# Expert routing shared out between GpSimd and VectorE, and weight pieces in other slots, in a two-layer transformer block

## What is computed

```python
x = x + linear_attention(layernorm(x))   # 16 heads of 8, causal
x = x + experts(layernorm(x))
x = x + softmax_attention(layernorm(x))  # 16 heads of 8
x = x + experts(layernorm(x))            # same weights as the first
```

```python
scores = sigmoid(x @ router_w.T)             # 16 per token
s = scores + bias
group_score = top_k(s.reshape(-1, 4, 4), 2).sum(-1)   # 4 groups of 4
gmask = the 2 groups with the highest group_score
idx = top_k(where(gmask, s, -1), 4)
w = scores[idx] / (sum(scores[idx]) + 1e-20) * 2.5
out = sum_e w_e * down_e(silu(x @ gate_e) * (x @ up_e)) + shared
```

## Time and profile before

| | us |
|---|---|
| median of 3 runs | 585.02 |
| lowest and highest | 580.65, 589.15 |
| the profiled execution | 585.89 |
| its span, first to last instruction | 584.2 |
| mean granted clock of TensorE (1 is 2.4 GHz) | 0.955 |
| busy in the span: TensorE, VectorE, ScalarE, GpSimd | 527.8, 439.5, 338.2, 313.0 |

### The profile page before, as it was taken

The page is one execution under the profiler, slowest core; times in us unless marked ns, Lnnn a source line. Parts: engine busy times, 40 slices in busy tenths (PEclk is TensorE's granted clock), DMA queues, the critical chain, the costliest instruction groups (busy, mean ns, idle before and its releaser), DMA issues. The chain is left out here.

```text
span 584.2 us, 11501 instructions
## 1 busy us (share of the span) xinstructions
PE 527.8 (90%) x3757; PEld 395.6 (68%) x3757; DVE 439.5 (75%) x1073; ACT 338.2 (58%) x575; POOL 313.0 (54%) x309
## 2 busy tenths in 40 slices
PE   4888677979999999999888898998999999999996
PEld 3655454667888888888555554655578888888884
DVE  3678679838889798667676787788578797886563
ACT  2566554456555655655455768576855655555553
POOL 4797784436665766677520303111165666656664
PEclk9999995989999999999867999989999999999999
DMA  6359761043353434335632432420153544355350
GB/s 176 100 164 279 226 212 43 4 92 97 102 112 125 128 89 125 90 114 174 205 108 73 138 117 91 127 74 2 39 109 88 121 127 122 101 143 128 91 147 24
DMA packets 48548, 67.59 MB, mean 116 GB/s; under 512 B 6625, under 2 KB 18930, under 8 KB 48498
## 3 DMA queue, kind: packets, MB, share of 16 engines
q1 hardware_dynamic: 45392, 66.47, 39.7%
q10 hardware_dynamic: 3106, 0.48, 0.5%
HBM read 53.56 MB, written 13.37 MB: 115 GB/s over the span
## 5 line engine op out<-in xcount | busy, mean ns | idle before, releaser
L649 POOL TENSOR_TENSOR KS<-PT,QS 128x512 fp32r<-128x512 f32 x144 | 186.0, 1292 | 118.5 <-ACT QS L841 106.5
L836 ACT ACTIVATE bank<-bank 128x512 f32<-128x512 f32 x128 | 74.5, 582 | 99.0 <-PE bank L861 98.5
L1562 DVE TENSOR_TENSOR PT<-CS,bank 128x512 f32<-128x512 f32 x128 | 87.4, 683 | 45.1 <-PE bank L861 44.6
L859 PE MATMUL bank<-XH,WH 128*128 128x512 f32 (+1 forms) x288 | 115.4, 401 | 1.9 <-DVE PT L1434 1.7
L861 PE MATMUL bank<-XH,WL 128*128 128x512 f32 (+1 forms) x288 | 112.8, 392 | 0.0
L860 PE MATMUL bank<-XL,WH 128*128 128x512 f32 (+1 forms) x288 | 112.7, 391 | 0.0
L1459 DVE TENSOR_REDUCE MEXP<-bank 128x4 f32<-128x1024 f32 x64 | 78.2, 1222 | 25.9 <-PE bank L971 25.3
L841 ACT ACTIVATE QS<-PT 128x512 fp32r<-128x512 f32 x144 | 90.2, 626 | 12.0 <-DVE PT L1567 11.4
L1567 DVE TENSOR_TENSOR PT<-PT,bank 128x512 f32<-128x512 f32 x128 | 88.0, 688 | 9.5 <-ACT bank L836 1.6
L756 ACT ACTIVATE PT<-bank 128x1024 f32<-128x1024 f32 x64 | 65.5, 1025 | 42.8 <-PE bank L1003 42.4
L1026 PE MATMUL bank<-PT,V 128*32 128x256 f32 (+1 forms) x1024 | 68.4, 389 | 2.4 <-DVE PT L1434 1.0
(11 more groups left out here) (186 smaller groups left out, 789.6 us busy)
## 6 DMA issues: line engine op xcount, KB each, us to landing
CS<-combine_rows SPq DMA_DIRECT2D x128, 256.0 KB, 3.2
...
```

The source lines that it names most:

```text
L649: pool.tensor_tensor(GL[:, (u - 1) % 3, :], GG[:, (u - 1) % 3, :], GH[:, (u - 1) % 3, :].bitcast(f32), ALU.subtract).then_inc(F.gl, 1)
L836: act.activation(TH[:, u, :] if u < SHARED else G[u % 3][:, :], G[u % 3][:, :], ACT.Silu).then_inc(F.th, 1)
L859: pe.matmul(out, wh, vh, start=start, stop=False)
L1562: dve.tensor_tensor(ab, CS[:, e % CBUFS, :], U[u % 3][:, :], ALU.mult).then_inc(F.b, 1)
```

## The change

`route` is now in two engines' queues. GpSimd has parts 0, 2, 3, 5 and 7 with the elementwise links, VectorE keeps parts 1 to 6 without them. Both wait for each other on the same semaphore. The scores plus bias are written into SB8, groups of 4 padded to 8 with a very low number, and 16 MAX8 on VectorE give the two largest of each of the 16 groups (4 groups in 4 tiles). Constants of two multiplications and an addition are now operands in memory (HALF, RSCALE). In front of two comparisons GpSimd multiplies one column into `pool_junk`. The pieces go to slots 9, 11, 15, 17, 23 and 25, for ScalarE and GpSimd alike.

```diff
-        PIECE_SLOTS = [9, 11, 16, 18, 24, 26]
+        PIECE_SLOTS = [9, 11, 15, 17, 23, 25]
-        ROUTE_SLOTS = [{24: (0,), 25: (1,), 26: (2,), 27: (3,), 28: (4,), 29: (5,), 30: (6,), 31: (7,)},
-                       {27: (0,), 28: (1,), 29: (2,), 30: (3,), 31: (4,), 32: (5,), 33: (6, 7)}]
+        POOL_ROUTE_SLOTS = [{24: (0,), 25: (2,), 27: (3,), 29: (5,), 30: (7,)},
+                            {27: (0,), 28: (2,), 29: (3,), 31: (5,), 32: (7,)}]
+        DVE_ROUTE_SLOTS = [{25: (1,), 26: (2, 3), 28: (4, 5), 30: (6,)},
+                           {28: (1,), 29: (2, 3), 30: (4, 5), 32: (6,)}]
-        ROUTE_AT = {False: {4: (0,), 5: (1,), 6: (2,), 7: (3,), 8: (4,), 9: (5,), 10: (6,), 11: (7,)},
-                    True: {0: (0,), 1: (1,), 2: (2,), 4: (3,), 6: (4,), 7: (5,), 8: (6, 7)}}
+        POOL_ROUTE_AT = {False: {4: (0,), 5: (2,), 7: (3,), 9: (5,), 11: (7,)},
+                         True: {0: (0,), 2: (2,), 4: (3,), 6: (5,), 8: (7,)}}
+        DVE_ROUTE_AT = {False: {5: (1,), 6: (2, 3), 8: (4, 5), 10: (6,)},
+                        True: {1: (1,), 3: (2, 3), 5: (4, 5), 7: (6,)}}
             def route_constants():
                 pool.memset(MEXP[:, :, :, :], 0.0)
+                pool.memset(SB8[:, :, :], -BIG)
+                pool.memset(HALF[:, :], 0.5)
+                pool.memset(RSCALE[:, :], ROUTE_SCALE)
+            def route(A, c, part):
+                base = c * LINKS
+                def link(k, instr):
+                    instr.then_inc(A.rv, 1)
+                def after(k):
+                    pool.wait_ge(A.rv, base + k)
+                by_group = SB8[:, :, 0:EPG]
+                if part == 0:
+                    pool.wait_ge(A.th, c + 1)
+                    link(1, pool.tensor_tensor(T4[:, :, :], TH64[:, bass.ds(c * CT, CT), :], HALF[:, 0:1].unsqueeze(2)
+                                               .broadcast_to([P, CT, EXPERTS]), ALU.mult))
+                    after(1)
+                    link(2, pool.tensor_tensor(SC[:, :, :], T4[:, :, :], HALF[:, 0:1].unsqueeze(2)
+                                               .broadcast_to([P, CT, EXPERTS]), ALU.add))
+                    after(2)
+                    link(3, pool.tensor_tensor(by_group.rearrange("p (t g) e -> p t g e", g=GROUPS),
+                                               SC[:, :, :].rearrange("p t (g e) -> p t g e", e=EPG),
+                                               RB[:, :].rearrange("p (g e) -> p g e", e=EPG).unsqueeze(1)
+                                               .broadcast_to([P, CT, GROUPS, EPG]), ALU.add))
+                if part == 2:
+                    after(4)
+                    link(5, pool.tensor_tensor(GE[:, :, 0:GROUPS], TOP[:, :, 0].rearrange("p (t g) -> p t g", g=GROUPS),
+                                               TOP[:, :, 1].rearrange("p (t g) -> p t g", g=GROUPS), ALU.add))
+                if part == 3:
+                    after(7)
+                    pool.tensor_tensor(pool_junk[:, :], NEG[:, 0:1], NEG[:, 0:1], ALU.mult)
+                    link(8, pool.tensor_scalar(GMK[:, :, :], GR[:, :, 0:GROUPS], -BIG / 3, None, ALU.is_lt))
+                    after(8)
+                    gmk = GMK[:, :, :].rearrange("p t g -> p (t g)")
+                    pool.tensor_tensor(T1[:, :], gmk, NEG[:, 0:1].broadcast_to([P, CT * GROUPS]), ALU.add)
+                    link(9, pool.tensor_tensor(T4[:, :, :].rearrange("p t (g e) -> p (t g) e", e=EPG), by_group,
+                                               gmk.unsqueeze(2).broadcast_to([P, CT * GROUPS, EPG]), ALU.mult))
+                    after(9)
+                    link(10, pool.tensor_tensor(ME[:, :, 0:EXPERTS].rearrange("p t (g e) -> p t g e", e=EPG),
+                                               T4[:, :, :].rearrange("p t (g e) -> p t g e", e=EPG),
+                                               T1[:, :].rearrange("p (t g) -> p t g", g=GROUPS).unsqueeze(3)
+                                               .broadcast_to([P, CT, GROUPS, EPG]), ALU.add))
+                if part == 5:
+                    after(12)
+                    pool.tensor_tensor(pool_junk[:, :], NEG[:, 0:1], NEG[:, 0:1], ALU.mult)
+                    link(13, pool.tensor_scalar(W[:, :, :], ER[:, :, 0:EXPERTS], -BIG / 3, None, ALU.is_lt))
+                    after(13)
+                    link(14, pool.tensor_tensor(W[:, :, :], W[:, :, :], SC[:, :, :], ALU.mult))
+                if part == 7:
+                    after(17)
+                    link(18, pool.tensor_tensor(RSM[:, :], RSM[:, :], RSCALE[:, :], ALU.mult))
+                    after(18)
+                    pool.tensor_tensor(C[:, :, :], W[:, :, :], RSM[:, :].unsqueeze(2).broadcast_to([P, CT, EXPERTS]),
+                                       ALU.mult).then_inc(A.ct, 1)
...
+                if part == 1:
                     dve.wait_ge(s_pc, 9)
...
                     after(3)
...
+                    dve.memset(route_junk[:, :], 0.0)
+                    for t in range(CT * GROUPS):
+                        i = dve.max(out=TOP[:, t, :], in_=SB8[:, t, :])
+                    link(4, i)
```

More of the change, by code:

```diff
@@ L204, in hybrid_block @@
         SC = sb("SC", [P, CT, EXPERTS])
-        SBI = sb("SBI", [P, CT, EXPERTS])
-        PMX = sb("PMX", [P, CT * GROUPS, 2])
-        PMN = sb("PMN", [P, CT * GROUPS, 2])
+        SB8 = sb("SB8", [P, CT * GROUPS, 8])
+        TOP = sb("TOP", [P, CT * GROUPS, 8])
+        HALF = sb("HALF", [P, 1])
+        RSCALE = sb("RSCALE", [P, CT])
+        pool_junk = sb("pool_junk", [P, 1])
         T1 = sb("T1", [P, CT * GROUPS])
-        T2 = sb("T2", [P, CT * GROUPS])
-        T3 = sb("T3", [P, CT * GROUPS])
         GE = sb("GE", [P, CT, GROUPS + 8 - TOP_GROUPS])
@@ L640, in slot @@
                                        ALU.subtract).then_inc(Lnext.xl, 1)
+                for part in POOL_ROUTE_SLOTS[k].get(n, ()):
+                    route(A, 0, part)
             def unit(k, c, u, cur, prev, more):
@@ L661, in unit @@
                                        ALU.subtract).then_inc(LN[2].xl, 1)
+                if more:
+                    for part in POOL_ROUTE_AT[prev].get(u, ()):
+                        route(AT[k], c + 1, part)
             layers(pool, slot, unit)
@@ L1333, in after @@
                     dve.wait_ge(A.rv, base + k)
[L1335 to L1336 removed]
+                if part == 1:
                     dve.wait_ge(s_pc, 9)
[L1338 to L1348 removed]
                     after(3)
[L1350 to L1352 removed]
+                    dve.memset(route_junk[:, :], 0.0)
+                    for t in range(CT * GROUPS):
+                        i = dve.max(out=TOP[:, t, :], in_=SB8[:, t, :])
+                    link(4, i)
                 if part == 2:
[L1354 to L1355 removed]
                     after(5)
[L1357 to L1358 removed]
+                    dve.memset(route_junk[:, :], 0.0)
+                    for t in range(CT):
+                        i = dve.max(out=GM[:, t, :], in_=GE[:, t, :])
+                    link(6, i)
+                if part == 3:
                     after(6)
@@ L1390, in route @@
                         i = dve.max(out=EM[:, t, :], in_=ME[:, t, :])
-                    link(13, i)
+                    link(11, i)
                 if part == 5:
-                    after(13)
+                    after(11)
                     dve.memset(route_junk[:, :], 0.0)
@@ L1511, in side_steps @@
                         norm_aggregate(Lnext, c - 2)
-                    for part in ROUTE_SLOTS[k].get(n, ()):
+                    for part in DVE_ROUTE_SLOTS[k].get(n, ()):
                         route(A, 0, part)
@@ L1580, in unit @@
                 if more:
-                    for part in ROUTE_AT[prev].get(u, ()):
+                    for part in DVE_ROUTE_AT[prev].get(u, ()):
                         route(AT[k], c + 1, part)
```

59 lines of the change are left out of this document (7 added, 52 removed).

## The result

The changed kernel takes 582.89 us (median of 20 runs, 576.35 to 586.46), the kernel before 585.02; the ratio is 0.993 (95% interval 0.9903 to 0.9958). Put on the chip once more among the experiments it gave 583.79 us and 0.9961 (0.9931 to 0.9992). Both are within 2%. The ratios leave out executions that took over 1.5% longer than the fastest of the same kernel, and the profiled execution of the changed kernel, 585.08 us, is one of those. I had said 581, from 575 to 587.5.

A forecast was written before the change was run, and what follows sets the result against it. Bound taken: TensorE waiting for VectorE's masks, held up by GpSimd's long operations through a shared port lock, plus a slow clock. Terms -4.5 + 0.3 - 0.4 + 0 = -4.6 us on 585.9 gave 581.3, said as 581, range 575 to 587.5.

The forecast's parts named there:

- Parts 1 and 2: Routing: links leave VectorE, whose 16 MAX8 and memset cost 1.2 us; GpSimd's small operations cost 4.65 us per routing.
- The line through three widths: GpSimd price estimate from 128x4, 128x256 and 128x512 mean times: 0.33 us for each 128x64 operation.
- Rival A: Small GpSimd operations are dear, so TensorE waits in the expert stage: 596 to near 625 us, chance 0.08.
- Part 3: First attention stage, slots 23 to 28: without the stalls the mask of slot 29 starts 4.5 us earlier.
- A clock at 0.50 past slot 26: Listed sign of being wrong: TensorE's granted clock stays at 0.50 beyond slot 26 of the first stage.
- rival B: GpSimd's queue replaces the lock in the first stage; gain shrinks to 1 to 2 us, 584.5 us, chance 0.22.
- Rival D: Blocking by the lock was coincidence; stalls return at the next instructions, about 586 us, chance 0.07.
- Part 4: Pieces in slots 15 and 17: GpSimd's longer queue delays TensorE's transpose, cost 0.3 us, bounds +0.3 to -1.1.
- The early transpose: Listed sign of being wrong: this TensorE transpose waits more than 3.4 us; it had been idle 3.07 us.
- Part 5: Second attention stage: VectorE loses links but gets MAX8; between -1.4 and +0.6 us, taken as -0.4.
- Part 6: Expert stage, six routings: units 0 to 8 have 6.8 us free on GpSimd for 4.65, so cost 0.
- The tightest place is part 0 in unit 0: Expert stage: GpSimd's low half there would end at 208.2, before TensorE reads it at 209.25.

The follow-up runs named there:

- e10: Kernel before, with only GpSimd's low halves of weight pieces 4 and 5 moved from slots 24 and 26 to 31 and 33; 579.17 us, ratio 0.9875.
- e13: Kernel before, with GpSimd's low halves of weight pieces 4 and 5 in slots 32 and 33; 579.43 us, ratio 0.991.
- e3: Kernel before, old piece slots, with VectorE's first-chunk routing of layer 0 starting three slots later, in slot 27; 582.61 us, ratio 0.992.
- e5: Changed kernel with the routing of the chunk-0 units put behind the norm steps; 580.21 us, ratio 0.985.
- e1: Kernel before, routing all on VectorE, with only the pieces moved to slots 9, 11, 15, 17, 23, 25; 580.54 us, ratio 0.9907.
- e2: Changed kernel with the pieces in the old slots 9, 11, 16, 18, 24, 26; 585.33 us, ratio 0.9958.
- e6: Changed kernel with GpSimd links in the attention stages only, the six expert-stage routings back on VectorE; 579.57 us, ratio 0.9891.
- e7: Changed kernel with 14 extra 128x64 GpSimd products, never read, in each of four expert-stage routings; 581.73 us, ratio 0.9911.
- e8: Changed kernel with the first attention stage's routing on GpSimd two slots later, VectorE's parts moved too; 582.09 us, ratio 0.9919.
- e12: Changed kernel with chunk-0 routing behind the norm steps and GpSimd's low halves of pieces 4 and 5 in slots 31 and 33; 580.48 us, ratio 0.9891.
- e4: Kernel before with VectorE's routing three slots later and the pieces in slots 9, 11, 15, 17, 23, 25; 579.79 us, ratio 0.9875.
- e11: The changed kernel measured and profiled once more, unchanged; 583.79 us, ratio 0.9961 to the kernel before.

## Why the prediction was right, and where not

The time came out near what was said (ratios 0.993 and 0.996, forecast 581 / 585 = 0.993), and in part by luck: the slots gave 0.6 us less than forecast, the first expert stage cost 1.4 us that I had put at nothing, and small gains elsewhere, some of them no larger than the scatter, made up for it.

*Parts 1 and 2, prices.* Right. GpSimd's groups in the changed kernel:

```profile
L591 POOL TENSOR_SCALAR W<-ER 128x64 f32<-128x64 f32 x8 | 3.0, 370 | 0.0
...
L598 POOL TENSOR_TENSOR C<-W,RSM 128x64 f32<-128x64 f32 x8 | 2.4, 294 | 0.6
```

The line through three widths gave 0.33 us, and the 128x64 links took 0.29 to 0.37, comparisons and four-column patterns included; part 0 took 1.1 us where I had 1.2, and 16 MAX8 took 1.19 where I had 1.2. Rival A is excluded. The Trainium skill's rule against elementwise work on GpSimd (GPSIMD Engine Reference, "Engine selection") is borne out in direction: the 128x64 addition of the bias takes 0.32 us on GpSimd and 0.23 on VectorE when nothing holds it (e10). The difference is far below the stalls that it is traded for.

*Part 3, slots 23 to 28: -4.5.* Measured -3.95 (20.9 to 16.95), and within 0.03 us the same in the five profiles with this schedule. The first hand-over went as laid out (slot 24 to 25 in 2.3 us instead of 5.2), then TensorE waited 1.1 us for the part multiply, where I had 1.2. The rest is 0.6 us longer than laid out. Up to slot 28 the masks came a little earlier, and the step from slot 28 to 29 took 4.2 us for 3.2 laid out, with the clock at 0.50. A clock at 0.50 past slot 26 was on my list of signs of being wrong, and it came, from 97.5 to 104.3 us: this much of rival B is so. The layout also leaves unsaid that 2.8 of the 3.95 us are the clock's and 1.2 idle time; TensorE's one long wait for each piece became several of 0.5 to 1.1 us. And I had not asked which of the two edits brings the gain. Pieces alone give -2.7, the routing alone -3.3, both together -3.95: two remedies for one stall, so they don't add up. Each is one profile, and equal code can differ by 1.4 us in this stretch (14.2 in e10, 15.6 in e13), but the ratios say the same: 0.9907 and 0.9958 alone, 0.993 and 0.9961 together. Rival D, that the blocking was coincidence, is excluded by e10 and e3.

*Part 4: +0.3.* Slots 15 to 24 take 28.3 us before and 27.0 to 29.0 with the new slots, mean 28.2 over nine profiles: nothing to measure. The early transpose waited 1.73 us in one profile of the changed kernel and 2.09 in the other, not 3.4.

*Part 5: -0.4.* Attention stage 2 took 126.7 and 124.6 us against 128.4. But six kernels that have the old code there range from 125.1 to 129.7 (mean 127.7), and eight with the new code from 124.6 to 128.3 (mean 126.3), so no more can be said than that the sign may be right.

*Part 6: 0, the step that failed.* "The tightest place is part 0 in unit 0": it was not. Those four routings cost nothing, with double the work even. The cost was in the chunk-0 units, which I had not laid out: the norm steps there stand behind part 2, part 2 waits for VectorE's MAX8, and TensorE's transpose waits 2.27 us instead of 0.62, 1.65 us more. I had named what is queued behind VectorE's new wait, but not what is queued behind GpSimd's. The first expert stage takes 166.9 us instead of 165.5, and e5 takes it back.

These two numbers can be compared because the clock did the same in both. In before, in both profiles of the changed kernel and in e1, e2, e5, e6 and e7 there is one short stretch at 0.50 at the start of the stage. With the norm steps late the stage then takes 166.85 to 167.05 us, otherwise 165.1 to 165.5. In e3, e8, e10, e12 and e13 the clock stays at 1.00 there, in e4 it is low only ahead of the stage (112 to 115 us; the stage starts at 120.3), and each of these has a stage shorter by some 1.5 us than its like: 163.7 to 164.0, and 165.3 in e8, which has the same 2.3 us wait. Before, then e8:

```profile
112.00:124.00 12.00, 8.50 (x96) 5.45 (x86) 6.03 (x20) 4.81 (x10) 3.05 (x6) 0.86 0.50 92
```

```profile
112.00:124.00 12.00, 8.29 (x80) 5.91 (x73) 5.93 (x23) 6.48 (x14) 3.70 (x7) 1.00 0.33 92
```

The second expert stage was not 0 either: it gained 0.6 us (172.2 to 171.6).

Sum by the profiles: -3.95, -0.3 (slots 29 to 34), +1.4, -0.6 and some -1 of the second attention stage, unsure, are about -4.5, near the 2 to 4 us of the two ratios.

What stays open: which of e1, e4, e5, e6 and e10 is best. All are faster than the kernel before, by 0.9 to 1.5%, and their intervals overlap. Against the changed kernel the clearest comparison is e10 with e11, from one session: 0.9826 to 0.9925 against 0.9931 to 0.9992, so e10 is faster. With the first measurement of the changed kernel (0.9903 to 0.9958) all five overlap. e10 is also the simplest, one list of slots and no routing on GpSimd. Why the granted clock falls in one execution and not in another after the same waits was not found either. e10 was profiled once, so the clock of 1.00 in its slots may be that execution's. A half-width piece in each of two slots was not tried.
